# Gated feed-forward behind a long convolution: turns inside the convolution, one rescale moved, a narrow multiply split, and the last tile shared out anew

## What is computed

```python
kernel = 2 * einsum('hn,hnl->hl', Cs, exp(dtA[:, :, None] * arange(L))).real
y = irfft(rfft(u_m, 2L) * rfft(kernel, 2L))[..., :L] + u_m * D[:, None]   # causal convolution
y = y * mask
# W[k, n] = q[k, n] * s[k // 128, n] - (z[k // 128, n] + 1) * s[k // 128, n], q and z are 4 bits
gate, up = y2 @ Wg, y2 @ Wu              # (2048, 1024) @ (1024, 2752)
inter = gate * sigmoid(gate) * up
out = x + (inter @ Wd).astype(float16)   # (2048, 2752) @ (2752, 1024)
```

## Time and profile before

| | |
|---|---|
| median of 3 runs | 1215.04 us (1213.88 to 1215.89) |
| the profiled execution, its own time | 1214.16 us |
| its span, first to last instruction | 1212.4 us |
| PE, PE weight load, DVE | 96%, 79%, 74% of the span busy |
| ACT, POOL | 70%, 17% |
| chain of waits | PE 89%, DVE 6% |
| mean granted clock of PE | 0.980 |

### The profile page before, as it was taken

One profiled execution on the slowest core, in us unless ns is written; L12 is line 12 of the kernel. 1 busy time (PEld: TensorE's weight loads), 2 busy tenths in 40 slices (PEclk: granted clock), 3 DMA queues, 4 the chain that ended last, 5 costly groups with the idle time before them and its releaser, 6 DMA issues.

```text
span 1212.4 us, 15497 instructions
## 1 busy us (share of the span) xinstructions
PE 1168.9 (96%) x5546; PEld 953.3 (79%) x5546; DVE 893.1 (74%) x961; ACT 852.3 (70%) x1398; POOL 208.0 (17%) x121
## 2 busy tenths in 40 slices
PE   4998999999999999999999999999999999999995
PEld 4898998688788788888788678788788787887873
DVE  7788724477777777777777788787777777777777
ACT  5532203988788788788787877778787887887862
POOL 0021100121111211211211851211211211211110
PEclk8898999999999999999999999999999999999996
DMA  8665867434434434334334255545334334334423
GB/s 290 234 234 183 288 210 245 119 98 103 117 94 115 109 92 120 104 96 122 103 91 112 64 189 143 177 154 159 105 91 120 102 96 120 98 103 112 142 70 139
DMA packets 148018, 165.61 MB, mean 137 GB/s; under 512 B 24854, under 2 KB 111062, under 8 KB 147686
## 3 DMA queue, kind: packets, MB, share of 16 engines
q1 hardware_dynamic: 147910, 164.59, 46.2%
q0 software_dynamic: 32, 0.03, 0.0%
HBM read 155.74 MB, written 11.64 MB: 138 GB/s over the span
## 4 chain that ended last, share of the span: by engine, by line
PE 89%; DVE 6%; DMA 1%; issue 1%; SPq 1%; ACT 1%; POOL 0%; DVEq 0%
PE pair L1097 27%; PE pair L1132 26%; PE pair L1114 25%; PE pair L1057 9%; DVE acc L905 1%; PE pair L1017 1%; DMA x_fin<-in_x_dram 1%; DVE p L662 1%; DVE y_nat L811 0%; PE pair L1037 0%; DMA u_all<-in_x_dram 0%; DVE s_r L662 0%; SPq L395 0%; PE pair L1147 0%; DVE q_in L916 0%
## 5 line engine op out<-in xcount | busy, mean ns | idle before, releaser
L905 DVE SCALAR_TENSOR_TENSOR acc<-pair,s_down,acc 128x1024 f32<-128x1024 f32 x336 | 430.6, 1283 | 214.3 <-PE pair L1132 213.7
L605 ACT ACTIVATE pair<-pair,ratio 128x512 f32<-128x512 f32 x616 | 383.3, 668 | 114.9 <-PE pair L1097 114.8
L624 ACT ACTIVATE pair<-pair,ratio 128x512 f32<-128x512 f32 x588 | 365.2, 661 | 131.3 <-PE pair L1114 131.3
L1097 PE MATMUL pair<-xs,wg 128*128 128x512 f32 x1408 | 390.4, 399 | 2.7 <-DVE sil L884 2.7
L1114 PE MATMUL pair<-xs,wu 128*128 128x512 f32 x1344 | 370.3, 397 | 2.0 <-DVE sil L889 1.9
L1097 PEld LDWEIGHTS pair<-xs,wg 128*128 128x128 f32 x1408 | 263.8, 189 | 69.3 <-ACT pair L605 7.4
L1114 PEld LDWEIGHTS pair<-xs,wu 128*128 128x128 f32 x1344 | 249.2, 189 | 70.2 <-issue 11.9
L1132 PE MATMUL pair<-mid_h,wd 128*128 128x512 f32 x704 | 278.5, 400 | 5.4 <-DVE acc L905 3.5
L1132 PE MATMUL pair<-mid_l,wd 128*128 128x512 f32 x672 | 266.6, 397 | 0.0
L492 POOL CAST mid_h<-sil 128x1024 fp32r<-128x1024 f32 (+1 forms) x44 | 46.3, 1051 | 858.4 <-DVE sil L889 843.3
L1132 PEld LDWEIGHTS pair<-mid_h,wd 128*128 128x128 f32 x704 | 133.8, 192 | 43.9 <-DVE acc L905 9.7
(11 more groups left out here) (146 smaller groups left out, 379.8 us busy)
## 6 DMA issues: line engine op xcount, KB each, us to landing
q_in<-rows_backwards SPq DMA_DIRECT2D x672, 64.0 KB, 2.3
z_in<-zeros_plus_one SPq DMA_DIRECT2D x130, 256.0 KB, 4.6
toep<-kernel_padded SPq DMA_DIRECT2D x64, 512.0 KB, 5.9
q_in<-_L_ffn_down_qweight_dram SPq DMA_DIRECT2D x42, 512.0 KB, 5.7
u_all<-in_x_dram SPq DMA_DIRECT2D x16, 512.0 KB, 8.9
x_fin<-in_x_dram SPq DMA_DIRECT2D x12, 512.0 KB, 8.1
out_dram<-x_fin SPq DMA_DIRECT2D x12, 512.0 KB, 6.9
q_in<-in_x_dram SPq DMA_DIRECT2D x4, 512.0 KB, 5.8
```

The lines of the kernel that those rows point to most:

```text
L605: act.activation(gate_ps[:, tb, :], gate_ps[:, tb, :], ACT.Copy, scale=ratio[:, 0, G * t + g:G * t + g + 1]).then_inc(gate_scaled, 1)
L624: act.activation(up_ps(tau)[:, tb, :], up_ps(tau)[:, tb, :], ACT.Copy, scale=ratio[:, 1, G * t + g:G * t + g + 1]).then_inc(up_scaled, 1)
L905: dve.scalar_tensor_tensor(out=acc[:, hid, :], in0=ps, scalar=scale, in1=acc[:, hid, :], op0=ALU.mult, op1=ALU.add).then_inc(down_taken, 1)
L1097: mm = pe.matmul(gate_ps[:, tb, :], w["g"][tau % 2][:, g, :], xs[:, part, g, 512 * tb:512 * tb + 512], start=g == 0 and part == 0, stop=pa ...
```

## The change

- **Start.** Row groups 13, 14 and 15 are turned after convolution groups 0, 1 and 2 instead of before group 0. `unpack_rows` moves from group 3 to group 6, `turn_scales` from behind group 4 to behind group 7, `take_scales` from group 5 to group 11, and SP's store of the zeros from its turn 5 to 7. SP waits for all splits of the first half before the first weight load, and for the scales before the third.
- **Tile 0.** DVE rescales the second half of `up`; ACT keeps the other three. Shift and centering of the three weights that are prepared in tile 0 are spread over steps 0 to 5.
- **Narrow multiply.** It is done in two halves, at step 7 of the narrow tile and ahead of that step's take. Shift and centering of weight `d` 21 move from step 0 of tile 22 to behind that take. PE does one `down` ahead of the first gate of tile 22, and this gate waits for each half by itself.
- **End.** The last tile's split is done by ACT (high) and DVE (low) in halves. The last down products are 16 products of 512 columns over four PSUM banks. DVE takes nine; seven are scaled by ACT into a buffer and added by POOL. Six of the eight x row blocks go through PE: x times the identity in f32, then the sums turned by a product with an f16 identity into the same PSUM bank; ACT copies the result. Two blocks are turned and added by DVE as before. The f32 identity is now kept through the kernel.

```diff
+LAST = TILES - 1
+BY_POOL = (0, 3, 5, 7, 9, 11, 13)
+THROUGH_PE = (0, 1, 2, 3, 6, 7)
...
 # SP
                 if g == NG - 4:
                     sp.wait_ge(k_mm, NCH)
+                    sp.wait_ge(x1_split, HALF_G)
                     sp.wait_ge(z_stored, 32)
...
             sp.wait_ge(x1_split, HALF_G)
+            sp.wait_ge(scales_ready, 1)
             load_weights("d", 0)
...
 # ACT
-                for tb in range(2):
+                for tb in range(2 if tau else 1):
                     act.wait_ge(up_mm, 2 * (G * full_before(tau) + g) + tb + 1)
...
+            for tb in range(2):
+                act.wait_ge(last_mid, tb + 1)
+                act.copy(mid_h[0:M_TAIL, LAST % 2, 512 * tb:512 * tb + 512], sil[0:M_TAIL, tb]).then_inc(last_high, 1)
+            for e in BY_POOL:
+                scale_last(e)
+                if e == 11:
+                    copy_sum(0)
+                if e == 13:
+                    copy_sum(1)
+            for tt in THROUGH_PE[2:]:
+                copy_sum(tt)
...
 # DVE
+            def scale_first_up(g):
+                dve.wait_ge(up_mm, 2 * g + 2)
+                dve.tensor_scalar(up_ps(0)[:, 1, :], up_ps(0)[:, 1, :], ratio[:, 1, g:g + 1], None, ALU.mult
+                                  ).then_inc(first_up_scaled, 1)
...
                 take_conv(g)
-                if g == 3:
+                if g == 6:
                     unpack_rows()
-                if g == 5:
+                if g == 11:
                     take_scales()
...
-                    if g == 0 and tau:
+                    if g == 0 and tau and tau != NT:
                         multiply(tau - 1)
+                    if g == G - 1 and tau == TAIL:
+                        multiply(tau)
+                    if g == G - 1 and tau == LAST:
+                        multiply_last(0)
+                        multiply_last(1)
                     n = G * tau + g - LAG
                     if n >= 0:
                         take_down(n // NH, n % NH)
+                    if g == G - 1 and tau == TAIL:
+                        shift("d", TAIL)
+                        center("d", TAIL)
...
+            take_down(LAST - 1, NH - 3)
+            dve.wait_ge(down_mm, down_at(LAST - 2, NH - 1) + 1)
+            split_last(0)
+            split_last(1)
+            take_down(LAST - 1, NH - 2)
+            take_down(LAST - 1, NH - 1)
+            for e in range(2 * NH):
+                if e not in BY_POOL:
+                    take_last(e)
+            for tt in (4, 5):
+                finish_last(tt)
...
 # PE
-            for g in range(10, NG):
+            for g in range(10, 13):
                 turn(g)
             for hc in range(NG // 4):
                 for q in range(4):
                     convolve(hc, q)
-                    if 4 * hc + q == 4:
+                    if 4 * hc + q < 3:
+                        turn(13 + q)
+                    if 4 * hc + q == 7:
                         turn_scales()
...
+            def rows_first(tt):
...
+                for i in range(2):
+                    pe.matmul(down_ps[tt % 2][:, i, :], ident[:], x_slot(1, tt)[:, 512 * i:512 * i + 512],
+                              start=True, stop=True)
...
+            down(LAST - 1, NH - 3)
+            down(LAST - 1, NH - 2)
+            for e in range(4):
+                down_last(e)
+            down(LAST - 1, NH - 1)
+            rows_first(0)
+            down_last(4)
+            down_last(5)
+            rows_first(1)
+            for e in range(6, 12):
+                down_last(e)
+            rows_second(0)
+            down_last(12)
+            down_last(13)
+            rows_second(1)
+            down_last(14)
+            down_last(15)
+            rows_first(2)
+            rows_second(2)
+            rows_first(3)
+            rows_second(3)
+            turn_last(4)
+            turn_last(5)
+            rows_first(6)
+            rows_second(6)
+            rows_first(7)
+            rows_second(7)
```

More of the change, by code:

```diff
@@ L142, with pool_before, dve_before @@
 LOAD_ORDER = load_order()
+LAST = TILES - 1
+BY_POOL = (0, 3, 5, 7, 9, 11, 13)
+THROUGH_PE = (0, 1, 2, 3, 6, 7)
+def pool_before(e):
+    return sum(v < e for v in BY_POOL)
+def dve_before(e):
+    return e - pool_before(e)
 def load_at(m, tau):
@@ L1093, in gate @@
                 for tb in range(2):
+                    if g == 0 and tau == NT:
+                        pe.wait_ge(mid_done if tb else narrow_first, tau if tb else 1)
                     if G * tau + g:
@@ L1135, in down, with down_last @@
                 mm.then_inc(down_mm, 1)
[L1137 to L1139 removed]
+            def down_last(e):
+                tb, hid = divmod(e, NH)
+                if hid == 0:
+                    pe.wait_ge(last_low, tb + 1)
+                if e == 0:
+                    pe.wait_ge(centered, load_at("d", LAST) + 1)
+                if e == 2:
+                    pe.wait_ge(last_mid, 2)
+                if e >= 4 and e - 4 in BY_POOL:
+                    pe.wait_ge(last_scaled, pool_before(e - 4) + 1)
+                elif e >= 4:
+                    pe.wait_ge(last_taken, dve_before(e - 4) + 1)
+                pe.matmul(last_ps(e), w["d"][LAST % 2][:, P * hid:P * hid + P],
+                          mid_h[:, LAST % 2, 512 * tb:512 * tb + 512], start=True, stop=True).then_inc(last_mm, 1)
@@ new lines, in taken_before, with rows_second @@
+            def taken_before(e):
+                pe.wait_ge(last_taken, dve_before(e))
+                pe.wait_ge(last_summed, pool_before(e))
+            def rows_second(tt):
+                taken_before(NH if tt < 4 else 2 * NH)
+                for hid in range(NH):
+                    mm = pe.matmul(down_ps[tt % 2][:, hid // 4, P * (hid % 4):P * (hid % 4) + P],
+                                   o16[:, hid, P * tt:P * tt + P], ident16[:], start=False, stop=True,
+                                   skip_group_check=True)
+                mm.then_inc(sum_mm, 1)
```

187 lines of the change are left out of this document (125 added, 62 removed).

## The result

The changed kernel takes **1200.36 us** (median of 4 executions, 1198.56 to 1202.42); the kernel before took 1214.76 beside it (4 executions). The ratio is 0.9878, 95% interval 0.9865 to 0.9891: 14.4 us or 1.2% faster. The profiled execution is the fastest of the four: it took 1198.56 us for a span of 1196.5 us, against 1214.16 and 1212.4.

What follows compares the result with a forecast made beforehand. TensorE, busy 96% of the span, was taken as the bound, with gains only in four short places: -1.1 - 2.9 - 1.5 - 3.4 = -8.9 us, giving 1205.7 us, range 1200.5 to 1211.5.

Steps and rivals of the forecast that it cites:

- A: The start, up to tile 0: earlier convolution and scales ready sooner, less moved turns and a clock drop; -1.1 us.
- D: The end after the last tile: takes by halves, six x row blocks through PE, earlier stores; -3.4 us.
- C: Passage from tile 21 to 22: split narrow multiply gains, shift and centering under POOL's splits lose; -1.5 us.
- B: Tile 0: DVE takes one of ACT's four rescales per group, so PE sets the pace; -2.9 us.
- the walk: Passage from tile 21 to 22: following DVE's and POOL's queues, tile 22's multiply ends at 710.2 or 711.2, not 711.68.
- Rival 1: Whole kernel, everything opens up: A -2.6, C -3.5, D -5.5, together -14.5 us, 1200 us; chance 0.14.
- Rival 2: The end gives nothing, PE becomes its bound: D +1, C 0, together -3.0 us, 1211.2 us; chance 0.19.
- Rival 4: Moved work meets other waits: A, C and D 0, -2.9 us, or within 0.2% of before (chance 0.05).
- Rival 3: PE stays at half clock for the whole end: D +12.6 us, slower, 1221 us; chance 0.06.

Runs made afterwards that it cites:

- again: The changed kernel run once more without any edit: 1199.97 us, ratio 0.9887 to the kernel before.
- r_start: The changed kernel with the whole start undone (turns ahead of the convolution, scale rows handled early as before): 1205.86 us, ratio 0.9908 to the kernel before.
- v_spread: The changed kernel with shift and centering of weight tile 21 in the first two groups of tile 22: 1200.55 us, ratio 0.9883 to the kernel before.
- r_tile0: The changed kernel with tile 0 undone (ACT rescales all four halves): 1203.41 us, ratio 0.9896 to the kernel before.
- r_pass: The changed kernel with the passage from tile 21 to 22 undone (narrow multiply, gate order, shift and centering): 1201.57 us, ratio 0.9887 to the kernel before.
- r_shiftd: The changed kernel with only the early shift and centering of weight tile 21 taken back: 1200.56 us, ratio 0.9873 to the kernel before.
- b_fill: The kernel before with matmuls that nobody reads in three of TensorE's waits: 1209.28 us, ratio 0.9949 to the kernel before.

## Why the prediction was too cautious

**The step that failed is the one on half clock, in A and in D, and what I left uncredited in C.** I took it that each wait of about 2 us drops TensorE's clock after the change as it did before ("The convolution will now pay all of it: +0.9"; "a drop to half clock, which costs 1.6 us as in the start"), and left the drop behind the fifth kernel multiply in place except in a bound. In the profiled execution after, none of the three came, and a fourth that the kernel before has, behind the up matmul, went too. The sum with what they cost is:

- A: -1.1 forecast; the load landed 0.4 us sooner than taken (38.10, not 38.5); the convolution's first records did not pay the 1.6 us of the drop (84.23 against the 86.3 forecast is both together, 2.1); and behind the fifth multiply the way to tile 0 is 91.13 us instead of 92.28, with 1.3 us of scale turns added to it: 2.45 us. -1.1 - 0.4 - 1.6 - 2.45 = -5.55, what was measured. That is a lucky execution: by the mean of the eight profiles with this start A is -4.5. The structural terms held: wait of 2.19 (forecast 2.1), DVE ready 20.6 us after taking the kernel (105.5 less 84.96, forecast 20.6). My bound of -2.6 credited 1.5 us for one drop, and slow matmuls stood behind both waits.
- D: -3.4 less the 1.6 charged is -5.0, measured -4.8. That this comes so close is in part luck, by two errors of opposite sign (below). The profiles where the clock did fall at 1175 (again, r_start, v_spread) show 33.05 to 33.24 us instead of 31.65: 1.4 to 1.6, the charged size. The wait for POOL's fourth sum was 0.87 (taken as 1.0), the last copy ended at 1193.04; with the 11.1 us by which the last gate moved that is 1204.1, forecast 1205.0. Without the 1.6 us the forecast would have been 1203.4, so the work in front of the last copy cost 0.7 us more than summed, and the stores behind it gave 1.0 (4.45 us from last add to end before, 3.47 after) instead of 0.4. The first error is in a sum of the prediction: six records in 1.40 us are 0.233 us each, so 512 columns cost 0.93, not 0.87, and a row block 1.87, not 1.75; they took 1.88 to 1.98.
- B: -2.9 forecast, -2.8 in the profile, 2.87 by r_tile0. The DVE rescale took 0.76 (taken as 0.69, bound 1.08), and PE set the pace.
- C: -1.5 forecast for the multiply's end; it ended at 701.89, which is 710.3 on the clock of before (8.4 us of A and B added). The number was right by luck: the walk had given 710.2 or 711.2, and the parts were others. The stall behind POOL came as forecast (shift and centering 2.90 and 3.21 us, and a wait of 3.27 on PE: right, "for 1.6 to 4 us"), but up to this landmark the runs make the passage's edits as a whole worth 0.15 us (r_pass): +1.55 and -1.40 (r_shiftd). The rest of the 1.4 was the clock, which the kernel before lost behind its wait of 2.74 us; b_fill's passage without that drop is 505.15 us (507.95 less the 2.8 of tile 0), near the changed kernel's 505.27. The changed kernel loses the clock there too, behind its wait of 3.27 (0.91 in the rows above), but nothing of it reaches the up matmul: r_tile0 has the same passage at a clock of 1.00 and comes to 505.34 (508.14 less 2.8). Another 1.3 us came behind the up matmul, where the wait shrank from 1.93 to 1.39 and the clock stayed up: 462.82 instead of 464.13, and still 1.6 with the wait for x rows taken off.
- The early shift and centering in C don't lose what they seem to: they cost 1.40 us ahead of the up matmul, and the shorter wait in front of it (1.39 instead of 2.40) spares the drop behind it. At the last gate, less the wait for x rows, all of the passage's edits are worth 1.6 us (968.9 for r_pass, 967.3), and the place of these two nothing (967.2 for r_shiftd).

Rival 1 (everything opens up: 1200, A -2.6, C -3.5, D -5.5) had the right total, and its first and last terms the right cause, but POOL and DVE did not miss each other in C and its A was too small; it got a chance of 0.14, so its total is in part luck. The row it was argued down with, a gap of 1.94 us that dropped the clock, was one sample: the same gap did and didn't in these runs. Rival 2 fell: PE, with the x rows on it, bounds the end and still finishes sooner. Rival 4 fell: A, C and D all gained. Rival 3 fell: in the eleven profiles with the new end the clock of 1175 to 1195 us is 1.00 seven times and otherwise 0.91 to 0.97, from one drop behind the wait of some 0.7 us. The Trainium skill's rule behind it (TensorE: Matmul & The Clock Gate, "A second HAM failure mode: psum-queue depth-cycling") is not what this end does: 1.00 with idle times of 0.69 to 1.37 us between its groups.

The Trainium skill's rule that I did use (SBUF — State Buffer, "SBUF: two separate sides") held again: shift and centering, begun under a POOL instruction, ended 0.55 and 1.1 us behind its end (679.38 against 678.83, 682.69 against 681.60), near their own 0.76 and 1.22, while the two takes behind them, which read PSUM and ran beside POOL's work from 682.61 on, took 2.46 us together, 1.23 each.

**What the clock is worth.** Of the 15.9 us of span, b_fill's profile (1207.8 against 1212.4) puts 4.6 on the clock without touching the order of work; from b_fill to the changed kernel it is 11.3 us, of which 1.3 or so is again the clock (b_fill's wait before the up matmul dropped it: the four records at 706.80 took 2.01 us instead of 1.17) and up to 1.6 at the end, where the new order would have lost that with a drop. So some 8.5 to 10 us are the change's own work and 6 to 7.5 the clock, an estimate from single profiles. By the ratio b_fill has 6.2. What the old end itself loses to its half clock is left in the 8.5 to 10, as b_fill's end has it too. In the turns alone it can be up to 1.4 us, if DVE waits for all of it: in the kernel before 32 turns took 3.59 us at a granted clock of 0.50, and the 16 behind them 1.07.

```profile
1196.89 3.59 PE L1147 MATMUL pair<-ident,o 128*128 128x128 f16 x32 [2.46 <-ACT o L640]
...
1201.23 1.07 PE L1147 MATMUL pair<-ident,o 128*128 128x128 f16 x16 [0.74 <-DVE x_fin L916]
```

**Open.** Why a wait of one length drops the clock in one execution and not in the next is not settled; the wait at the fifth multiply is 2.19 us with both outcomes. The Trainium skill has a rule that would fit (TensorE: Matmul & The Clock Gate, "What's actually happening"): the chip judges TensorE's activity in windows that run on by themselves and don't start with the kernel, so that the same kernel gets its clock at another place in another run. By it, a wait drops the clock or not by where it falls; the runs agree in that both happen, and no view shown here has the windows themselves. The clock says much of how long an execution takes: again's six go from 1198.15 us at 0.994 to 1206.51 at 0.986, and 1199.35 at 0.996. The range of a kernel like this has to hold both.

## What to carry to other kernels

Price a wait on TensorE as its idle time plus a chance of the slow matmuls behind it; here a wait of 0.7 to 3.5 us cost either itself, or itself and 1.3 to 2.5 us more where PE was the bound behind it (and nothing more in the changed passage, where DVE was). When a change shortens waits, credit that second part where the trace before shows slow matmuls behind them, and give the range both cases; when it only moves work beside a POOL instruction, look for what DVE then stands under. Part of the change can look harmful at one landmark and be neutral at the next, so compare at more than one. One profile of each side can't tell a gain of the order from luck with the clock: compare distances between landmarks, and read the granted clock of each stretch first.

## What had not been expected of the hardware

- The same wait with and without a drop of the clock: 2.19 us, then 1.20 or 1.92 us for the kernel multiply; ahead of the convolution waits of 1.73 to 1.95 us (five profiles), then 4.79 us for the 32 records, and waits of 1.57, 1.63 and 2.09 us, then 6.43 to 6.46 us; 2.90 us in r_pass without a drop.
- Useless matmuls in three waits made the kernel before 6.2 us faster (ratio 0.9949).
- Bringing a 128x1024 x row block into PSUM by f32 matmuls with the identity, four records of 512 columns, took 1.88 to 1.98 us at full clock (forecast 1.75), beside POOL sums of 1.27 and DVE takes of 0.69 for 128x512.
- PE's wait for a down buffer under DVE's x rows is 0 to 2.8 us in kernels with the same code there, a second source of scatter beside the clock.
